# A transformer block on one core: stacked projections written to HBM as rows and loaded in three transfers, maxima in twos in the FFN's slots, output projection and second FFN in one program

## The reference

```python
x = h
x = x + 0.5 * ffn(layernorm(x))
x = x + attention(layernorm(x))      # causal, softmax over 2048 keys, then @ Wo.T + bo
x = x + 0.5 * ffn(layernorm(x))      # same FFN weights: gelu(gate) * up, then down
```

## Time and profile before

| | |
|---|---|
| median of 3 runs | 1220.93 us (1220.8 to 1222.6) |
| the profiled execution | 1220.02 us, its span 1218.3 us |
| TensorE, share of the span busy | 91% |
| VectorE, ScalarE, GpSimd | 57%, 47%, 9% |
| mean granted TensorE clock | 0.954 |
| transfers | 37.43 MB in 69331 packets |

### The profile page before, as it was taken

The page is one execution under the profiler, slowest core; times in us unless marked ns, Lnnn a source line. Parts: engine busy times, 40 slices in busy tenths (PEclk is TensorE's granted clock), DMA queues, the critical chain, the costliest instruction groups (busy, mean ns, idle before and its releaser), DMA issues. The chain is left out here.

```text
span 1218.3 us, 18414 instructions
## 1 busy us (share of the span) xinstructions
PE 1113.4 (91%) x6464; PEld 721.1 (59%) x6464; DVE 694.4 (57%) x1604; ACT 575.6 (47%) x1114; POOL 112.0 (9%) x409
## 2 busy tenths in 40 slices
PE   5999999988977769889999999999966999999997
PEld 3888888866854323333333333333255888888886
DVE  6976445454453336758888888888235333333333
ACT  5654434422414524655677776767742222222222
POOL 1000000000001112322111111111130000000000
PEclk9999999998988757999999999999987999999999
DMA  6010100220100320221111111010000000000000
GB/s 179 2 31 1 44 27 1 72 60 1 44 27 9 98 60 27 62 64 35 48 34 32 33 49 48 23 29 1 2 13 0 1 1 18 1 17 0 17 0 17
DMA packets 69331, 37.43 MB, mean 31 GB/s; under 512 B 47418, under 2 KB 63106, under 8 KB 69250
## 3 DMA queue, kind: packets, MB, share of 16 engines
q1 hardware_dynamic: 69249, 36.39, 11.1%
HBM read 25.63 MB, written 10.49 MB: 30 GB/s over the span
## 5 line engine op out<-in xcount | busy, mean ns | idle before, releaser
L1001 ACT ACTIVATE attn_prob<-psum 128x512 f32<-128x512 f32 (+3 forms) x640 | 298.3, 541 | 173.0 <-PE psum L693 172.6
L1139 DVE TENSOR_REDUCE attn_part_max<-psum 128x1 f32<-128x512 f32 x384 | 242.1, 684 | 60.7 <-PE psum L708 59.7
L752 PE MATMUL psum<-attn_prob,attn_vals 128*32 128x512 f32 (+3 forms) x1280 | 163.7, 565 | 3.1 <-POOL attn_prob L538 3.1
L605 PE MATMUL psum<-ffn_xt,all_w_hi 128*128 128x512 f32 x512 | 166.2, 406 | 0.0
L1273 PE MATMUL psum<-ffn_xt,all_w_hi 128*128 128x512 f32 x512 | 162.8, 399 | 2.5 <-DVE ffn_xt L1354 2.5
L1360 DVE TENSOR_TENSOR ffn_inner<-ffn_act_out,ffn_inner 128x512 fp32r<-128x512 f32 x64 | 44.3, 692 | 167.3 <-ACT ffn_inner L1324 167.3
L1142 DVE CUSTOM_DVE_ANT_0 attn_junk<-psum,attn_mask 128x128 bf16<-128x128 f32 (+3 forms) x256 | 117.1, 485 | 32.8 <-PE psum L708 32.3
L1332 ACT ACTIVATE ffn_act_out<-psum 128x512 f32<-128x512 f32 x64 | 38.2, 598 | 185.5 <-PE psum L1273 185.5
L620 PE MATMUL psum<-all_w_hi,ffn_inner 128*128 128x256 f32 x512 | 107.9, 294 | 0.1
L1273 PEld LDWEIGHTS psum<-ffn_xt,all_w_hi 128*128 128x128 f32 x512 | 92.6, 190 | 21.8 <-issue 2.9
L605 PEld LDWEIGHTS psum<-ffn_xt,all_w_hi 128*128 128x128 f32 x512 | 93.4, 194 | 17.2
(11 more groups left out here) (133 smaller groups left out, 1593.1 us busy)
## 6 DMA issues: line engine op xcount, KB each, us to landing
qk_parts<-qkv_parts SPq DMA_DIRECT2D x16, 384.0 KB, 2.5
all_x<-in_L_attn_h SPq DMA_DIRECT2D x4, 512.0 KB, 6.2
v_rows<-qkv_rows_v SPq DMA_DIRECT2D x16, 128.0 KB, 2.6
attn_vals<-v_rows SPq DMA_DIRECT2D x8, 256.0 KB
out<-all_x SPq DMA_DIRECT2D x4, 512.0 KB, 2.9
attn_q_early<-qk_parts SPq DMA_DIRECT2D x16, 96.0 KB
attn_q_late<-qk_parts SPq DMA_DIRECT2D x16, 96.0 KB
attn_k_mid<-qk_parts SPq DMA_DIRECT2D x6, 192.0 KB
```

What stands on the lines that cost most here:

```text
L605: last = nc.tensor.matmul(psum[:, 2 * m + q % 2, :], w_part[a][:, 3 * g + m, pl, o:o + P], xt[:, b % 2, c, pl, :], start=(n == 0), stop=(n ...
L752: last = nc.tensor.matmul(psum[r:r + 32, O0, at:BT], vals[:, k0 * SUB + kb + k, 2 * hd:2 * hd + 32], prob[:, (4 * d + 2 * k + hd) % PRING, ...
L1001: nc.scalar.activation(prob[:, n % PRING, at:BT], psum[:, S0 + n % SBANKS, at:BT], ACT.Exp).then_inc(s["exp"], 1)
L1139: nc.vector.tensor_reduce(to, psum[:, bank, :], AX.X, ALU.max).then_inc(s["max_read"], 1)
```

## The change

**Rows in HBM.** `qk_parts` becomes `qk_rows`, [2, 16 heads, 96, 2048]: the 96 rows of a head as the tile wants them, each part as often as it is used. `out_part` issues three transfers for a unit, with 3, 2 and 1 copies (a source that repeats for Q, fewer parts for K); it writes 768 KB where 384 KB were written. `load(n)` is then three transfers: queries of both heads, keys of both heads, values. The values' transfer is the same.

**Order.** `load(2)` is issued when the last unit and rows of V are made, ahead of the last two `out_part`; `load(3)` behind these instead of in the steps. Block 3's turn, units and rows stand at steps 1, 3, 4 and 5, one at a time between scores. `chunk_steps` follows `quota`: 3 chunks a step for d = 8 to 11, 7 in 3 steps up to d = 47, then 2 a step as before, and a chunk may stand 4 steps behind `free_at` instead of 6. The groups' turns move: group 7's from step 17 to 19, one ahead of its first score at step 20; groups 4 and 5 stay one step ahead; group 9 has two. From step 49 on the plan is as before.

**Maxima in twos.** In block 3 a slot's maxima stand two ahead of `gate_up(b, q, 0)`, two ahead of `gate_up(b, q, 1)`, and the rest behind it. VectorE reads the first two ahead of `low_part`, the others ahead of `product`.

**One program behind attention.** `back` holds the output projection and the second FFN, without loops. Wo and bo are loaded at the start of the Q, K, V phase, bo is added to x by GpSimd at steps 20 to 23 (`add_bias`), the heads are turned from where they are, the norms are made block by block, and `down`, the last addition and the store are signalled in halves. Blocks 2 and 3 are added (`join`) in the FFN's first two steps.

```diff
+            def quota(d):
+                return 0 if d < 8 else 3 * (d - 7) if d < 12 else 12 + (d - 11) * 84 // 36 if d < 48 else 96 + 2 * (d - 47)
...
+                at = [-2] * (N_EARLY // 2)
+                for i, (g, _, _) in enumerate(chunks[N_EARLY // 2:]):
+                    d = next(d for d in range(NS) if quota(d) > i)
+                    at.append(max(d, at[-1], free_at(g // 2) + 4))
+                return at
...
             EARLY_SLOTS = {1: 6, 2: 6, 3: 6, 4: 6, 11: 5, 12: 5, 13: 5, 14: 5, 15: 4}
-            EARLY_TURNS = {5: 0, 11: 1, 14: 2}
+            EARLY_TURNS = {4: 0, 12: 1, 13: 2}
             early, early_at = [], {}
...
+                mine = []
+                for k in range(EARLY_SLOTS.get(q, 0)):
+                    mine.append(len(early))
+                    early.append(("max", sum(1 for u in early if u[0] == "max")))
+                early_at[q] = [mine[0:2], mine[2:4], mine[4:]]
+                if q in EARLY_TURNS:
+                    early_at[q][2].append(len(early))
                     early.append(("turn", EARLY_TURNS[q]))
...
+            LAST_UNITS = {(3, 1): 0, (4, 1): 1, (5, 1): 2, (5, 3): 3}
+            LAST_ROWS = {(3, 3): (0, 1), (4, 3): (2, 3)}
...
-                            sp.dma_start(qk_dram[NPART * kind:NPART * (kind + 1), half * P:(half + 1) * P, b * BT:(b + 1) * BT]
-                                         .rearrange("a p t -> p a t"), parts[:, u % 2, :, :]).then_inc(s[f"part_out{u % 2}"], 16)
+                            to = qk_dram[kind, half * 8:half * 8 + 8, :, b * BT:(b + 1) * BT].rearrange("h (d j) t -> (h d) j t", j=len(Q_PARTS))
+                            for k, (at, copies) in enumerate(((0, 3), (3, 2), (5, 1))):
+                                mine = parts[:, u % 2, k:k + 1, :].broadcast_to([P, copies, BT]) if kind == 0 else parts[:, u % 2, 0:copies, :]
+                                sp.dma_start(to[:, at:at + copies, :], mine).then_inc(s[f"part_out{u % 2}"], 16)
...
-                                j, n, part = ((0, 3, 0), (3, 2, 1), (5, 1, 2))[j]
-                                sp.dma_start(queries(b, hd)[j * HD:(j + n) * HD, :], qk_dram[part, own, qt * BT:cols].unsqueeze(0).broadcast_to(
-                                                 [n, HD, 2 * BT])).then_inc(s[f"stack{b}"], 16)
-                            else:
-                                j, n = ((0, 3), (3, 2), (5, 1))[j - 3]
-                                sp.dma_start(keys(k0, hd)[j * HD:(j + n) * HD, 0:qt + 2, :].rearrange("p c t -> p (c t)"),
-                                             qk_dram[NPART:NPART + n, own, 0:cols]).then_inc(s[f"stack{b}"], 16)
+                            sp.dma_start(queries(b)[0:KR, :, :], qk_dram[0, 2 * p:2 * p + 2, :, qt * BT:cols].rearrange("h r t -> r h t")
+                                         ).then_inc(s[f"stack{b}"], 16)
+                            sp.dma_start(keys(k0)[0:KR, :, 0:qt + 2, :].rearrange("p a c t -> p a (c t)"),
+                                         qk_dram[1, 2 * p:2 * p + 2, :, 0:cols].rearrange("h r t -> r h t")).then_inc(s[f"stack{b}"], 16)
+                            sp.dma_start(vals[:, k0 * SUB:(k0 + qt + 2) * SUB, 1:1 + 2 * HD], v_dram[p, :, 0:SUB * (qt + 2), :]
+                                         ).then_inc(s[f"stack{b}"], 16)
                         def max_row(g):
...
+                        sp.wait_ge(s["unit"], NU * NB)
+                        sp.wait_ge(s["v_sum"], SUB * NB)
+                        load(2)
+                        for n in (2, 3):
                             out_part(NU * (NB - 1) + n)
-                        sp.wait_ge(s["rest"], NU * NB)
-                        sp.wait_ge(s["v_sum"], SUB * NB)
-                        for j in range(LOADS):
-                            load(2, j)
-                        out_part(NU * NB - 1)
+                        load(3)
                         outs_landed(NB - 1)
                         constant_rows(k_mid)
                         constant_rows(k_late)
...
                         for d in range(NS):
+                            if 20 <= d < 20 + NB:
+                                add_bias(d - 20)
                             for g in range(EARLY, NG_A):
...
+                                if b == NB - 1:
+                                    for u in early_at[q][0]:
+                                        early_step(u)
                                 gate_up(b, q, 0)
                                 if n is not None:
                                     turn_scales(n)
+                                if b == NB - 1:
+                                    for u in early_at[q][1]:
+                                        early_step(u)
                                 gate_up(b, q, 1)
                                 if b == 0 and q == 14:
                                     turn(F_USE[1])
...
+                                if (d, j) == (1, 2):
+                                    turn(Q_USE[NB - 1])
+                                if (d, j) in LAST_UNITS:
+                                    unit(NU * (NB - 1) + LAST_UNITS[d, j])
+                                if (d, j) in LAST_ROWS:
+                                    for i in LAST_ROWS[d, j]:
+                                        rows_of_v(SUB * (NB - 1) + i)
                                 if j == 2 and gathered(d) is not None:
                                     gather(gathered(d))
...
-                            elif d <= 4:
-                                project(NB - 1, d - 1)
                         weigh(NS - 1)
                         gather(NG_A - 1)
...
-                                if d == 1 and j == 1:
+                                if (d, j) == (1, 1):
                                     split(Q_USE[NB - 1])
-                                if 2 <= d <= 6 and j == 1:
-                                    projected(NB - 1, d - 2)
+                                if (d, j) in ((4, 0), (5, 0), (6, 0), (6, 2)):
+                                    second_part(NU * (NB - 1) + {4: 0, 5: 1, 6: 2}[d] + j // 2)
+                                if (d, j) in ((3, 2), (4, 2), (5, 2), (6, 0)):
+                                    take_unit(NU * (NB - 1) + d - 3)
```

Of `back`, the turn of the heads, the projection, and the order on TensorE and then on VectorE:

```diff
+                        def turn_heads(b):
+                            if b >= 2:
+                                pe.wait_ge(s["ot_lo"], b - 1)
+                            for pl in range(PL):
+                                for i in range(SUB):
+                                    last = nc.tensor.transpose(psum[:, TURN_BANK[b] + pl, i * P:(i + 1) * P],
+                                                               heads[:, b * SUB + i, pl::PL], ident[:, :])
+                            last.then_inc(s["o_turned"], 1)
...
+                        turn_weight()
+                        turn_heads(0)
+                        turn_heads(1)
+                        project(0)
+                        turn_heads(2)
+                        project(1)
+                        turn_heads(3)
+                        project(2)
+                        project(3)
+                        turn(0)
...
+                        dve.wait_ge(s["wt_hi"], 1)
+                        nc.vector.tensor_tensor(wt_o[:, 1, :, :], psum[:, 3, :].rearrange("p (l c) -> p l c", l=PL), as_f32(wt_o[:, 0, :, :]),
+                                                ALU.subtract).then_inc(s["wt_lo"], 1)
+                        split_heads(0)
+                        split_heads(1)
+                        join(0)
+                        variance(0)
+                        split_heads(2)
+                        join(1)
+                        norm(0)
+                        split_heads(3)
+                        split(0)
```

528 lines of the change are left out of this document (230 added, 298 removed).

## The result

The changed kernel takes 1143.26 us (median of four runs, 1142.83 to 1144.71), the one before 1221.49 in the same series: a ratio of 0.9361, with a 95% interval of 0.9345 to 0.9377. I forecast 1158 and a range of 1144 to 1176. The direction was right; the gain is 78 us where I had 62, and the time lies just outside the range. The profiled execution (1144.71 us, span 1142.6) is 75.7 us shorter in span than the one of before.

A forecast was written before the change was run, and what follows sets the result against it. TensorE, busy 91% of the span, was taken as the bound, with idle time and half clock to recover. Gains 17 + 15 + 12 + 18.5 = 62.5 from 1220.0 gave 1157.5; the median stands 0.9 higher: 1158, range 1144 to 1176.

The forecast's parts named there:

- Slots: Block 3 of the first FFN: half a gate_up covers a pair's reading; 12 us idle and 5 of half clock go, -17.
- Writing the rows: Sixteen units issue three transfers for one, 384 KB more; counted 0, or 3 us in the attention steps if cover failed.
- steps 0 to 7: First attention steps: same matmuls and ScalarE passes in fewer steps; 0, between -4 and +4.
- Steps 8 to 11: Attention: the wait for pair 2's load goes, three chunks a step; 34.2 us becomes 19, -15.
- The rule behind the load: DMA loads: slowest dimensions set how many of 16 engines work; 96-long transfers use sixteen, so rows stop queueing behind loads.
- Steps 12 to 47: Attention: fourteen chunks in six steps take 19.6 us, plus 4 for rows and 3 for clock; -12.
- third rival: Half clock stays through steps 8 to 20 because three one-step stalls come close together; about 10 us, 1168, 10%.
- Additions: GpSimd's additions moved to steps 20 to 23: neither masks nor VectorE delayed, 0; 9.93 us by a lock on everything.
- Output projection: From last heads to the second FFN's first gate_up: projection, turns and norms block by block; -15, between -7 and -17.
- Second FFN: Second FFN: less half clock 1.5, no drain at the pass's end 1, additions and store in halves 1 us; -3.5.
- Fifth: Rival: all stalls smaller and clock up; block 3 -22 and steps 8 to 47 -34, 1146, 14%.
- That the slots gain little: Rival in block 3: each pair waits for VectorE as the six did; the stretch gives 5, 1170, 12%.

The follow-up runs named there:

- sixes: Changed kernel with each slot's early maxima in one group again, behind gate_up's second half, and VectorE reading them behind its product; 1172.63 us.
- twos, behind: Changed kernel with maxima in twos kept, but VectorE reading the second and third pair behind the product instead of ahead; 1163.66 us.
- sixes, ahead: Changed kernel with all nine slots' early maxima in one group behind gate_up's second half, VectorE reading them ahead of the product; 1158.66 us.
- before, ahead: Kernel before the change, with VectorE in block 3 reading a slot's maxima ahead of the product instead of behind it; 1211.55 us.
- threes: Changed kernel with each slot's early maxima in two groups of at most three, VectorE reading ahead of the product; 1150.36 us.
- sixes in slots 1 to 4: Changed kernel with early maxima in one group in slots 1 to 4 alone, in twos in slots 11 to 15; 1147.91 us.
- narrow form: Changed kernel with every load in five transfers, the source of queries and keys written as 3 x 32 rows, slowest dimension 3 instead of 96; 1227.47 us.

## Why the prediction was wrong in size

**Slots.** This is the step that failed: a term of the sum that was too small, 17 us for 26.3. The idle time fell by 13.8 us (19.6 to 5.8; in the sum 12), so "I leave as waits: 7 in all" held. The rest of the term did not: "With two thirds of the idle time gone I give back 5" was 12.5, read as TensorE's busy time in block 3 (102.7 to 90.2). Two things were wrong in it. First, half clock does not go in proportion to idle time. All kernels of this block side by side, idle time and time at half clock: 21.5 and 20.4 us (sixes), 19.6 and 20.4 (before), 18.9 and 17.0 (twos, behind), 13.6 and 10.2 (sixes, ahead), 12.7 and 10.2 (before, ahead), 11.1 and 3.4 (threes), 8.0 and 6.8 (sixes in slots 1 to 4), 5.8 and 0 (changed; 5.9 and 3.4 in the runs with the same slots). With two thirds of the idle time gone at least five sixths of the half clock is. The 3.4 us make block 3 of the changed kernel's profiled execution 1.5 us shorter than in eight of those runs; that much of the 9 us is luck. Second, 12.5 us of busy time went and not the 8 of my 20 x 0.84 / 2. TensorE was busy for 19.8 of the 20.4 us at half clock, so the clock accounts for 9.9. The rest goes with the size of the groups: less half of what was busy at half clock, block 3 has 92.8 to 93.4 us of busy time in the four kernels with nine groups of six, 91.7 with four such groups, 91.1 with threes and 90.0 to 90.6 with twos. Why larger groups keep TensorE busy longer is not shown.

**The reason for the slots was half a reason.** I compared a pair's reading (1.37 us) with half a gate_up (1.41) and took the sharing of two banks for the cause of the waits. The order on VectorE, which I never weighed, is worth 11.8 us of block 3 with groups of six and 20 to 22 with twos; the grouping is worth 6.1 with the reading behind the product and 14 to 16 with it ahead. The timeline of before had it: the 2.01 us that the product waits for gelu, ahead of the readings.

**Writing the rows, steps 0 to 7.** Counted 0; the stretch gained 1.2 us, which no run explains.

**Steps 8 to 11.** Right: -16.9 for -15, the load in time, one wait of 2.12 us where I had put 2. The rule behind the load was the right ground: with a narrow form and all else as changed, pair 2's load takes 14 us from its first issue to its last update, as in the kernel before, and the stretch 33.3 us. That narrow transfers can also hold SP at its next issue, the prediction did not have.

**Steps 12 to 47.** The pace was right (steps 24 to 47: 19.8 us for six, 19.6 forecast; a third way between two and three chunks). The waits and the clock behind them cost 10 us in steps 12 to 23 (49.3 us for the 39.2 of the pace alone), where I left 7 for all 36 steps. That the three one-step stalls and the half clock come together was my third rival; the run with the turns a step sooner shows its price, 10.5 us for waits of 5.0.

**Additions.** Counted 0; with them at steps 100 to 103 the time is the same, 1143.27 us.

**Output projection.** -18 for -15. I put the first projection at half clock (5.6 us); it took 3.13. The other items came within a microsecond.

**Second FFN.** -6.7 for -3.5. The pass's end gave 1.8 (I had 1). The end of the kernel gave more than my 1: from the end of the last gate_up to the end of the span 7.9 us instead of 11.0, since besides the addition and the store in halves the last two `down` no longer wait 0.62 and 0.40 us for low parts. In the old order ScalarE makes a gelu ahead of the high part of the step before, which would make them late; no run tries that alone. The first block gives 0.8, and the stretch from block 2's middle to the last gate_up 1.0.

**The rivals.** Fifth (stalls smaller, clock up, 1146) came nearest by its time, through block 3 and not through steps 8 to 47 (-24.8, less than the forecast's 27). That the slots gain little, that rows stay behind loads (the bytes set the landing) and that the additions disturb is refuted; the third, half clock behind the one-step stalls, came true in part. The range ended 2 us below the fifth rival's value, too near for a term whose clock part I had capped at 8. The time lies less than 1 us outside it only because steps 12 to 47 gave 4 us less than forecast, against 9 more in block 3, 3 each in the projection and the second FFN, and 2 in steps 8 to 11.

## What to carry to other kernels

Where two engines hand banks to each other, read the order on the receiving engine as well: an instruction ahead of the reading that waits for a third engine delays it as much as a missing buffer does. Where waits come close together, idle time of TensorE cost up to twice its length (27.8 us of block 3 for 15.6 of idle time, 10.5 us for 5.0 of waits for rows; with threes only 6.3 us for 5.3, against the 97.6 us of the other runs), so price a stall by its length and the half clock that the profile shows around it. Write a DMA's slowest dimension as long as the partitions it fills; in transfers of 192 to 384 KB a rearranged source of the same bytes cost 84.6 us.

## What was unexpected of the hardware

Transfers whose source begins with 3 can hold the issuing queue: behind those of 192 to 384 KB a 24 KB issue took 4.87 us, a pair of 3 KB rows 6.01 us and a single row up to 11.9 us, where they take 0.77, 1.50 and at most 0.78 else. Behind the smaller ones of the kernel before no issue of a row was held, and two other issues took 2.5 and 7.0 us. What sets the limit is not shown. A written-out loop was no faster than the looped one (1166.84 and 1167.17 us).
